# Norms by logarithm and exponential on ScalarE, biases folded into centred weights, bits by two signs, row maxima stored by elements

## What is computed

```python
def attn(x, Wq, bq, Wv, bv, hyperplanes):            # H = 16, NB = 64, NH = 6
    q = (x @ Wq.T + bq).reshape(B, S, H, Dh)
    v = (x @ Wv.T + bv).reshape(B, S, H, Dh)
    proj = einsum('bshe,en->bshn', concat([q, ones]), hyperplanes)
    buckets = einsum('bshn,n->bsh', (proj >= 0), 2 ** arange(NH))
    scores = einsum('bhsd,bhtd->bhst', q, q) / sqrt(E)
    same = (b_hs[:, :, :, None] == b_hs[:, :, None, :])
    attn = softmax(scores * (NB - 2 + same), axis=-1)
    return einsum('bhst,bhtd->bhsd', attn, v)

def ffn(x, ...):                                      # 128 -> 512 -> 512 -> 512 -> 128
    h = silu(tlin(x, w1)) * tlin(x, w2)
    h = gelu(tlin(h, h1)); h = gelu(tlin(h, h2))
    return tlin(h, w3)

x = x + layernorm(attn(layernorm(x)))
x = x + layernorm(ffn(layernorm(x)))
```

## Time and profile before

| | us |
|---|---|
| median of 3 runs | 1377.42 |
| lowest and highest run | 1373.04, 1378.29 |
| span of the profiled execution | 1378.0 |
| first score tile on DVE, last subtraction on POOL ends | 29.7, 1304.6 |
| DVE's first score tile of batch 3 and of batch 15 (12 batches, 78.95 each) | 265.1, 1212.5 |

### The profile page before, as it was taken

One profiled execution on the slowest core, in us unless ns is written; L12 is line 12 of the kernel. 1 busy time (PEld: TensorE's weight loads), 2 busy tenths in 40 slices (PEclk: granted clock), 3 DMA queues, 4 the chain that ended last, 5 costly groups with the idle time before them and its releaser, 6 DMA issues. The chain is left out here.

```text
span 1378.0 us, 19641 instructions
## 1 busy us (share of the span) xinstructions
PE 1223.5 (89%) x5302; PEld 500.2 (36%) x5394; DVE 1225.7 (89%) x3837; ACT 1084.6 (79%) x1573; POOL 1221.7 (89%) x259
## 2 busy tenths in 40 slices
PE   3666799999989999998989999998999999898897
PEld 1211234343333434333343434433343433333343
DVE  4988999999999999999999999999999999999420
ACT  2344778979797988979798897979798897979852
POOL 2699999999999999999999999999999998999810
PEclk9877999999999999999999999999999999999998
DMA  3563445444544455455544544454454535453100
GB/s 104 154 182 112 132 111 154 127 130 120 147 120 118 132 134 141 109 140 125 131 133 124 142 123 132 133 139 129 114 136 128 145 98 146 120 135 102 40 8 8
DMA packets 89470, 167.37 MB, mean 121 GB/s; under 512 B 18192, under 2 KB 54160, under 8 KB 89360
## 3 DMA queue, kind: packets, MB, share of 16 engines
q1 hardware_dynamic: 89252, 165.82, 44.6%
q10 hardware_dynamic: 108, 0.30, 0.1%
HBM read 150.59 MB, written 15.47 MB: 121 GB/s over the span
## 5 line engine op out<-in xcount | busy, mean ns | idle before, releaser
L980 POOL TENSOR_TENSOR logits<-max_row,logits 128x4096 f32<-128x4096 f32 x128 | 1138.7, 8915 | 65.6 <-DMA max_row<-max_scratch 41.0
L808 DVE CUSTOM_DVE_ANT_0 logits<-s_bank,coeff 128x512 f32<-128x512 f32 x1024 | 692.5, 676 | 0.0
L1032 ACT ACTIVATE logits<-logits 128x1024 f32<-128x1024 f32 x512 | 509.0, 1048 | 44.8 <-POOL logits L980 43.6
L758 DVE TENSOR_SCALAR coeff<-brow,bcol 128x516 bf16<-128x516 bf16 x1024 | 485.2, 474 | 36.8 <-PE s_bank L550 31.2
L550 PE MATMUL s_bank<-mov_stack,stat_stack 128*128 128x512 bf16 x932 | 324.8, 393 | 42.4 <-DVE rowmax L808 31.7
L570 PE MATMUL aux_bank<-logits,v_pad 128*32 128x512 f32 x2048 | 255.3, 618 | 39.8 <-ACT logits L1032 38.9
L701 PE MATMUL f_bank<-hid_b,h_sb 128*128 128x512 f32 x512 | 249.0, 594 | 0.9
L690 PE MATMUL f_bank<-hid_a,h_sb 128*128 128x512 f32 x512 | 246.1, 592 | 0.1
L550 PEld LDWEIGHTS s_bank<-mov_stack,stat_stack 128*128 128x128 bf16 x1024 | 93.2, 99 | 317.7 <-DVE rowmax L808 177.8
L690 PEld LDWEIGHTS f_bank<-hid_a,h_sb 128*128 128x128 f32 x512 | 96.0, 190 | 80.6 <-issue 69.3
L701 PEld LDWEIGHTS f_bank<-hid_b,h_sb 128*128 128x128 f32 x512 | 95.0, 190 | 80.8 <-issue 70.9
(11 more groups left out here) (101 smaller groups left out, 911.5 us busy)
## 6 DMA issues: line engine op xcount, KB each, us to landing
max_row<-max_scratch SPq DMA_DIRECT2D x128, 512.0 KB, 4.2
brow<-bucket_scratch SPq DMA_DIRECT2D x63, 522.0 KB, 6.3
mov_stack<-q_scratch SPq DMA_DIRECT2D x192, 96.0 KB
stat_stack<-q_scratch SPq DMA_DIRECT2D x189, 96.0 KB
max_scratch<-rowmax_T SPq DMA_DIRECT2D x512, 1.0 KB
q_scratch<-q_parts SPq DMA_DIRECT2D x16, 384.0 KB, 4.6
x_in<-in_x SPq DMA_DIRECT2D x16, 256.0 KB, 3.1
q_scratch<-q_parts SPq DMA_DIRECT2D x16, 256.0 KB, 5.1
```

The source lines that it names most:

```text
L758: nc.vector.tensor_scalar(coeff[:, k % 3, :].rearrange("p (r n) -> p r n", r=ROW_RUNS), brow[:, h // 4 % 2, h % 4, :, 0:RUN], bcol[:, b % ...
L808: nc.vector.tensor_tensor_reduce(out=logits[:, ring(b, k), :], in0=tile_bank(k)[:], in1=coeff[:, k % 3, 0:SEQ], scale=float(E) ** -0.5, sc ...
L980: nc.gpsimd.tensor_tensor(tiles, max_row[:, m % 2].unsqueeze(2).broadcast_to([P, GROUP, ST, SEQ]), tiles, ALU.subtract).then_inc(below_max ...
L1032: nc.scalar.activation(logits[:, first:first + 2, :], logits[:, first:first + 2, :], ACT.Exp, scale=-1.0).then_inc(probs_done, 1)
```

## The change

It has these parts.

- Row maxima: no transpose; SP stores the 128x8 tile with one DMA whose destination has the 8 values of a partition 128 floats apart. DVE's wait for the transpose of two groups ago becomes a wait for that group's store.
- Softmax sums: `invert_sums` on ACT takes a logarithm of the sums and the exponential of its negative; DVE only multiplies.
- Norms: reciprocal standard deviations are exp(-0.5 ln(var + eps)) on ACT. For x, POOL multiplies the bias from it; for the attention output DVE does, from a copy that ACT writes to PSUM; y1 needs no bias any more, as w1 and w2 are centred.
- Weights: Wq and Wv (and later w1 and w2) are multiplied by a centring matrix at the start, and bq and bv are added to every row as b/128; since xnT is stored plus 1.0, the product gives x W + b. The q copies and the value copy need no bias; the value copy moves from DVE to ACT.
- Bits: ACT takes sign(proj + bias), then sign(2 s + 1), giving -1 and 1; `weights16` is as before.
- Tables: the set that holds both logarithm and exponential is named at the start and after each pair of silu or gelu.
- The bucket row matmul writes all 128 partitions instead of 16 (the weights are padded with zeros).
- Many slots are changed by a few places.

```diff
-X_STATS_SLOT = 3
-LATE_X_STATS_SLOT = 33
-X_MOMENTS_SLOT = 24
-X_PREPARE_SLOT = 26
-X_RSTD_SLOT = 40
-X_NORM_SLOT = 49
+X_STATS_SLOT = 5
+LATE_X_STATS_SLOT = 36
+X_MOMENTS_SLOT = 20
+X_PREPARE_SLOT = 24
+X_BIAS_SLOT = 43
+X_NORM_SLOT = 47
...
-DIVIDE_LAGS = (39, 40)
-V_ADD_SLOT = 32
-PROJ_SLOT = 25
-BITS_SLOT = 26
-BCOL_SLOT = 28
-END_PREPARE_SLOT = 49
-END_RSTD_SLOT = 56
-SUB_SLOT = 13
-EXP_SLOTS = (13, 13, 14, 16)
-STORE_SLOT = 4
-LOAD_SLOT = 6
-Q_STORE_SLOT = 34
-ROW_STORE_SLOT = 41
+RDEN_LAG = 37
+DIVIDE_LAG = 39
+V_ADD_SLOT = 30
+PROJ_SLOT = 26
+BITS_SLOT = 23
+BCOL_SLOT = 29
+END_PREPARE_SLOT = 51
+SUB_SLOT = 14
+EXP_SLOTS = (13, 14, 14, 15)
+STORE_SLOT = 0
+LOAD_SLOT = 4
+Q_STORE_SLOT = 30
+ROW_STORE_SLOT = 53
...
             def store_maxima(b, m):
-                sp.wait_ge(rowmax_T_done, b * GROUPS + m + 1)
-                for n in range(MAXIMA_DMAS):
-                    sp.dma_start(max_scratch[b, m * GROUP:(m + 1) * GROUP].rearrange("h (t s) -> (h t) s", t=ST)[:, 32 * n:32 * (n + 1)],
-                                 rowmax_T[32 * n:32 * n + GT, m % 2, :]).then_inc(maxima_stored, 16)
+                sp.wait_ge(logits_done, b * TILES + (m + 1) * GT)
+                sp.dma_start(max_scratch[b, m * GROUP:(m + 1) * GROUP].rearrange("h (t s) -> s (h t)", t=ST),
+                             rowmax[:, m % 2, :], allow_slow_non_contiguous=True).then_inc(maxima_stored, 16)
...
+            for n, (weights, shift) in enumerate(((wq_sb, bq_sb), (wv_sb, bv_sb))):
+                nc.tensor.matmul(f_bank[n][:, 0:E], centre, weights[:], start=True, stop=False)
+                nc.tensor.matmul(f_bank[n][:, 0:E], even_row[:], shift[:], start=False, stop=True).then_inc(centred_psum, 1)
...
-                nc.vector.transpose(rowmax_T[:, m % 2, :], rowmax[:, m % 2, :]).then_inc(rowmax_T_done, 1)
...
-                    dve.wait_ge(rowmax_T_done, n // GT - 1)
+                    dve.wait_ge(maxima_stored, 16 * (n // GT - 1))
...
-                    nc.vector.scalar_tensor_tensor(out=aux_bank[:], in0=aux_bank[:], scalar=bq_sb[:],
-                                                   in1=q_parts[:, 0, :], op0=ALU.add,
-                                                   op1=ALU.subtract).then_inc(q_part_steps, 1)
+                    nc.vector.tensor_tensor(aux_bank[:], aux_bank[:], q_parts[:, 0, :],
+                                            ALU.subtract).then_inc(q_part_steps, 1)
...
-                nc.gpsimd.tensor_tensor(out_[:], var[:], minus_half[:], ALU.pow).then_inc(done, 1)
-                nc.gpsimd.tensor_tensor(bias[:], shift[:], out_[:], ALU.mult).then_inc(bias_done, 1)
...
+            def rstd(var, scale, log, out_, ready, count, log_done, done, n):
+                act.wait_ge(ready, count)
+                nc.scalar.activation(log[:], var, ACT.Ln, bias=eps[:], scale=scale).then_inc(log_done, 1)
+                act.wait_ge(log_done, n)
+                nc.scalar.activation(out_[:], log[:], ACT.Exp, scale=-0.5).then_inc(done, 1)
...
+            def invert_sums(b, pair):
+                sums = aux_bank[:].rearrange("p (t h w) -> p t h w", t=ST, w=HALF_W)[:, :, :, DH:DH + 1]
+                done = b * PAIRS + pair
+                act.wait_ge(o_psum, done + 1)
+                nc.scalar.activation(den_log[:].unsqueeze(3), sums, ACT.Ln).then_inc(den_log_done, 1)
+                act.wait_ge(den_log_done, done + 1)
+                if done:
+                    act.wait_ge(att_done, done)
+                nc.scalar.activation(rden[:], den_log[:], ACT.Exp, scale=-1.0).then_inc(rden_done, 1)
...
+                if k == V_ADD_SLOT:
+                    nc.scalar.copy(
+                        v_pad[:, p % 2, :, 0:PAD_PITCH - HALF_W].rearrange("p r (h w) -> p r h w", w=VW)[:, :, :, 0:DH],
+                        projection_bank(p, 1)[:].rearrange("p (r h d) -> p r h d", r=2 * ST, d=DH)).then_inc(v_added, 1)
+                if k == BITS_SLOT:
+                    nc.scalar.activation(bitsT[:], projection_bank(p, 0)[0:NH * H, :], ACT.Sign,
+                                         bias=hbias_sb[:]).then_inc(signs_done, 1)
+                    act.wait_ge(signs_done, p + 1)
+                    nc.scalar.activation(bitsT[:], bitsT[:], ACT.Sign, bias=1.0, scale=2.0).then_inc(bits_done, 1)
...
+            def att_scale(f):
+                nc.scalar.activation(att_log[:], att_mv[:, :, 1], ACT.Ln, bias=eps[:]).then_inc(att_log_done, 1)
+                act.wait_ge(att_log_done, f + 1)
+                nc.scalar.activation(normed_bank(f)[:, 0:ST], att_log[:], ACT.Exp, scale=-0.5).then_inc(att_rstd_done, 1)
+                nc.scalar.activation(att_rstd[:], att_log[:], ACT.Exp, scale=-0.5).then_inc(att_scale_done, 1)
...
+                if k == ATT_BIAS_SLOT:
+                    dve.wait_ge(att_rstd_done, f + 1)
+                    nc.vector.scalar_tensor_tensor(out=att_bias[:], in0=att_mv[:, :, 0], scalar=-1.0, in1=normed_bank(f)[:, 0:ST],
+                                                   op0=ALU.mult, op1=ALU.mult).then_inc(att_bias_done, 1)
...
-                    nc.scalar.activation(end_std[:], end_sum[:], ACT.Sqrt, bias=eps[:],
-                                         scale=1.0 / E).then_inc(end_std_done, 1)
+                    rstd(end_sum[:], 1.0 / E, end_log, end_rstd, end_square_done, (f + 1) * ST, end_log_done, end_rstd_done,
+                         f + 1)
...
+                        nc.scalar.preload_act_table_set(EXP_LOG_TABLE)
```

More of the change, by code:

```diff
@@ L293, in sandwich_kernel @@
         o_psum = sem("o_psum")
+        den_log_done = sem("den_log_done")
         rden_done = sem("rden_done")
@@ L726, in iteration @@
                     pe.wait_ge(ffn_in, 16 * FFN_DMAS)
+                    pe.wait_ge(brow_done, i + 1)
+                    for n, weights in enumerate((w1_sb, w2_sb)):
+                        nc.tensor.matmul(f_bank[n][:], centre, weights[:], start=True,
+                                         stop=True).then_inc(ffn_centred_psum, 1)
                 for k in range(TILES):
@@ L1022, in _ @@
         def _(act):
-            act.wait_ge(consts_made, 4)
-            nc.scalar.activation(table_warm[:], ident[:, 0:1], ACT.Exp)
+            nc.scalar.preload_act_table_set(EXP_LOG_TABLE)
+            act.wait_ge(consts_made, CONSTS)
             act.wait_ge(projection_in, 16 * PROJECTION_DMAS)
+            for n, weights in enumerate((wq_sb, wv_sb)):
+                act.wait_ge(centred_psum, n + 1)
+                nc.scalar.copy(weights[:], f_bank[n][:, 0:E]).then_inc(projection_centred, 1)
             def exponential(b, m, n):
@@ L1052, in copy_output @@
                 nc.scalar.copy(oT[:], aux_bank[:]).then_inc(oT_done, 1)
+            def invert_sums(b, pair):
[7 more added lines that the diff above has]
+                nc.scalar.activation(rden[:], den_log[:], ACT.Exp, scale=-1.0).then_inc(rden_done, 1)
             def query_step(p, k):
                 if k == x_slot(p, X_PREPARE_SLOT, LATE_X_PREPARE_SLOT):
-                    prepare(x_mv, x_var, x_shift, x_mv_done, x_var_done, p + 1)
+                    act.wait_ge(x_mv_done, p + 1)
+                    nc.scalar.activation(x_shift[:], x_mv[:, :, 0], ACT.Identity, scale=-1.0).then_inc(x_shift_done, 1)
+                    rstd(x_mv[:, :, 1], 1.0, x_log, x_rstd, x_mv_done, p + 1, x_log_done, x_rstd_done, p + 1)
                 if k == X_NORM_SLOT:
+                    act.wait_ge(x_rstd_done, p + 1)
                     act.wait_ge(x_bias_done, p + 1)
-                    normalise(x_in, x_in, x_rstd, x_bias, xn_done)
+                    for t in range(ST):
+                        last = nc.scalar.activation(x_in[:, t, :], x_in[:, t, :], ACT.Identity, bias=x_bias[:, t:t + 1],
+                                                    scale=x_rstd[:, t:t + 1])
+                    last.then_inc(xn_done, 1)
                 if k == XNT_COPY_SLOT:
@@ L1064, in query_step @@
                         act.wait_ge(v_psum, p)
-                    nc.scalar.copy(xnT[:], aux_bank[:]).then_inc(xnT_done, 1)
+                    nc.scalar.activation(xnT[:], aux_bank[:], ACT.Identity, bias=1.0).then_inc(xnT_done, 1)
                 if k == Q_HIGH_SLOT:
@@ L1166, in iteration @@
                     act.wait_ge(ffn_in, 16 * FFN_DMAS)
+                    for n, weights in enumerate((w1_sb, w2_sb)):
+                        act.wait_ge(ffn_centred_psum, n + 1)
+                        nc.scalar.copy(weights[:], f_bank[n][:]).then_inc(ffn_centred, 1)
                 for k in range(TILES):
@@ L1172, in iteration @@
                         copy_output(b, pair)
+                    for b, pair in pairs_at(i, k, RDEN_LAG, attend, feed):
+                        invert_sums(b, pair)
                     if project:
```

283 lines of the change are left out of this document (129 added, 154 removed).

## The result

The changed kernel takes 1942.4 us (median of 4 runs, 1937.05 to 1943.97) against 1377.55 us before: a ratio of 1.409, 95% interval 1.406 to 1.412. The forecast was 1338 with a range of 1315 to 1386. It was wrong in its sign, and by more than 600 us in size.

A forecast was written before the change was run, and what follows sets the result against it. No engine was far ahead, but DVE, least idle, was taken to end most waits. 1.64+1.1-0.4 = 2.3 us a batch, 37 over 16, plus 2.5 at the end, off 1378.0 gave 1338 us; range 1315 to 1386.

The forecast's parts named there:

- The path of the row maxima: From DVE's maxima through SP's store to their load: 1.3 us saved, elements cost 1.0, so 0.3 shorter, counted as nothing.
- Rival (d): Element store lengthens POOL's waits, three a batch, against 3.4 us freed; 1.5 us more path gives 1394 us; chance 0.11.
- The far bound of +4.8 us: Largest lengthening of the maxima's path, with 64 elements for each DMA engine at the q store's 96 ns, 6.1 us.
- That DVE ends the wait: DVE, least idle at 2.7 us a batch, ends the wait in most stretches; the change takes 3.8 us off it.
- the loose stretches all and the tight ones half: DVE savings count fully where PE idles (stretches 5-7, 1.64 us), half where PE is nearly full (1.1 of 2.16).
- ACT's added work: Bits, value copy, inversions and norms add 1.4 us a batch to ACT, one table load saved; bounds 0.2 and 2.7.
- loads near 192: Sign to look for in the profile after: the number of ACT table loads near 192.
- ACT's place in the chain: One uncovered inversion of sums on ACT delays the exponentials PE's value matmuls wait for: 0.4 us a batch, between 0 and 1.4.
- rival (c): Nothing measurable: late bits, two ACT activations behind exponentials, hold PE another 0.7 us a batch; 1373 us; chance 0.10.
- The slots that SP's transfers were moved past: SP's row store, moved behind the sixth group: its landing wait lies within eight tiles (8.6 us or more) before the next store.
- rival (e): Named table set isn't kept; some ten loads of 1.28 us a batch on ACT, above 1420 us; chance 0.02.
- The end and the start: Centring matmuls at the start cost nothing, at most 2 us; norms and a table load at the end save 2.5 us.

The follow-up runs named there:

- the kernel before with runs of 32 bytes: Kernel before, only the maxima store changed: no transposes, one DMA of 128 runs of 32 bytes (maxima in wrong places); 1362.2 us, ratio 0.9866.
- the last kernel: Changed kernel with transposes, bits, sums and value copy back on DVE, bucket row early, next x loaded before the maxima store; 1365.8 us, ratio 0.9901.

## Why the prediction was wrong, point by point

**The path of the row maxima** is the step that failed. It gave the elements 1.0 us with bounds of 0 and 6.1, on top of the 1.16 us that a landing took. SP now waits 10.7 us for the landing, 9.5 more, which is outside even the far bound. The bounds came from the wrong side. bq's 128 elements of 4 bytes are written into SBUF, one for each partition, and the q store writes rows of 1 KB; no row of the trace showed small writes into crowded DRAM. For elements far apart the price was near (28 ns, taken as 16; x_in gave 33). What was missing was a term for the place, 3.9 us for near elements and more for those side by side. Rival (d), with a chance of 0.11, named the mechanism, its point of decision (1.1 us on the path) and the sign by which to know it (POOL's waits). From last maximum to load the path grew by 11.3 us (2.9 to 14.2), not by 1.5: the landing, less the three issues saved, and another 2 us by which SP itself comes late to the store. That SP's queue would run out of time was nowhere in the sum; the prediction looked only at what stands behind one store and found it covered. It also held DVE's wait for the store of two groups ago to be covered, which came to 111.4 us. By (d)'s own rule of three waits a batch 11.3 us are 3 x 11.3-3.4 = 30.5 us a batch, 490 in all; the batch grew by 34.2 (78.95 to 113.15), as nearly every group waited (107 of 128). The far bound of +4.8 us that the prediction wrote down itself gives by the same rule 3 x 4.8-3.4 = 11 us a batch and 1552 us. So the rival's time of 1394 was too low, the range had to take in that bound and did not, and even the bound fell short.

**That DVE ends the wait** is supported by the kernel before with runs of 32 bytes: 19 us (13 to 24) for eight transposes a batch and the shorter path. The sum had 8 x 0.201, of which the loose stretches all and the tight ones half, 1.1 us a batch and 18 in all. The total is right by luck: two errors cancel. Durations overstate, since DVE's instructions overlap here by 0.07 to 0.09 us each. Timeline of DVE before, around a transpose:

```profile
716.19 0.48 DVE L758 TENSOR_SCALAR coeff<-brow,bcol 128x516 bf16<-128x516 bf16 x1
716.58 0.68 DVE L808 CUSTOM_DVE_ANT_0 logits<-s_bank,coeff 128x512 f32<-128x512 f32 x1
...
717.19 0.48 DVE L758 TENSOR_SCALAR coeff<-brow,bcol 128x516 bf16<-128x516 bf16 x1
717.58 0.20 DVE L768 STREAM_TRANSPOSE rowmax_T<-rowmax 128x32 f32<-128x32 f32 x1
717.71 0.65 DVE L808 CUSTOM_DVE_ANT_0 logits<-s_bank,coeff 128x512 f32<-128x512 f32 x1
```

Without a transpose the two instructions start 0.39 us apart, with it 0.52, and these are the medians of the whole trace: it costs 0.13, not 0.20 us. Eight are 1.04 us, 17 us in all, and the steady batch became 1.08 us shorter. So no half was lost in the tight stretches, unless the shorter path made up for it. In the changed kernel the same step, from transposes to runs of 32 bytes, is worth 25 us by the ratios (1.0147 to 0.9964).

**ACT's added work** was forecast at 1.4 us a batch, with one table load of 1.28 saved. The page of the kernel with transposes kept has 1121.4 us of ACT, 37 more than before, 2.3 a batch, inside the bounds of 0.2 and 2.7. The difference is the saved load: the trace before has 196 loads (88+31+31+29+16+1) and the changed one 193, so 3 were saved and not 16. The sign that was given, loads near 192, came true and says nothing, as it was not compared with the 196. But the larger error is that the sum charged only 0.4 us for ACT's place in the chain. That was the second failed step. By the ratios, the bits cost 6 us in all where they stand, the sums 10, the values 7, each although DVE was spared their work; and the two signs (0.666 and 0.630 us) stand where rival (c) had them, holding PE for 1.7 us a batch. The forecast had placed the bits in the 4.44 us that ACT idles in the third stretch. ACT reached them in the fourth, where it had 0.35 us to spare: in the kernel with transposes kept the first sign starts in every steady batch while DVE is at tile 28, five tiles past `BITS_SLOT = 23`. An engine does not reach a slot at the time at which another does.

**The slots that SP's transfers were moved past** were read only for the row store. The load of x, moved by one slot behind the store that moved by four, cost 7 and 10 us in two kernels by the ratios, together with the residual's load, which had come to stand in the same way at the sixth group.

**The table set** did what it says, with 193 loads in all; rival (e), some ten more a batch, is out. **The end and the start** (2.5 us less) were not measured apart.

So the rest of the change was forecast at 1356 us with the transposes (1338 and the 18 us that the sum gave them), a ratio of 0.984, and came to 1.0147, 42 us more. From there to the last kernel (0.9901) the undoings give back 34: sums 10, x 7, values 7, bits 6 and the bucket row 4, the last not told from nothing. The other 8 remain open. The undoings were made one on top of the other, so each number holds for its place in that order.

## What to carry to other kernels

A DMA's price has to be read from a row of the same direction and the same crowding: here small writes close together in DRAM cost several times what their count said, and a range has to hold the far bound that one's own rows give. Ask, too, whether the queue that waits for the landing has the time. On engines that run in order, ask of each moved step which longer steps it now stands behind and who waits for it, DMA issues included: here three moves that took work off the engine with the least idle time made the kernel slower, by 6 to 10 us each. Price a step by what it adds between the starts of its neighbours, where the trace shows that (0.13 us here), and not by its duration (0.20).

## What the hardware showed that was not expected

The landing of one DMA of 4 KB out of 128 partitions into DRAM took 1.4 us as 128 runs of 32 bytes, 3.2 as 1024 elements 512 bytes apart, 7.1 as 1024 elements 8 bytes apart; for elements 4 bytes apart, with neighbours from all partitions, SP waited 10.7 us. The packets themselves stayed short, 9 ns each. Other transfers of the same queue land late meanwhile (x_in 11.4 instead of 3.1 us in the changed kernel). And PE, which idled more, ran at a mean granted clock of 0.868 instead of 0.975, with the matmuls of the second hidden layer at 644 ns on average instead of 594.
